# A post-norm decoder layer on one core: key scores and turned-x casts reordered in the first unit of each attention batch

## The reference

```
kv = ln(x) @ kv_w + kv_b ; q = ln(x) @ q_w + q_b      # 16 heads of 32
q, k = rotary(q), rotary(k)                           # radius from x @ rh_w
qn, kn = ln(q), ln(k)                                 # per head
attn = softmax(qn @ kn^T / sqrt(32)) ; a = attn @ v
x = layernorm(x + a @ out_w + out_b)
x = layernorm(x + retention(x, ctx))                  # second phase
x = layernorm(x + coupling_ffn(x))                    # third phase
```

## Time and profile before

| | |
|---|---|
| median of 3 runs | 2026.33 us (2024.2 to 2029.24) |
| the profiled execution | 2028.34 us, of which the span of instructions is 2026.5 us |
| busy share of the span | PE 87%, DVE 73%, ACT 62%, POOL 43% |
| attention, retention, coupling phase | about 1070, 470 and 486 us |
| mean granted clock of TensorE | 0.95 of full speed |

### The profile page before, as it was taken

One profiled execution on the slowest core, in us unless ns is written; L12 is line 12 of the kernel. 1 busy time (PEld: TensorE's weight loads), 2 busy tenths in 40 slices (PEclk: granted clock), 3 DMA queues, 4 the chain that ended last, 5 costly groups with the idle time before them and its releaser, 6 DMA issues. The chain is left out here.

```text
span 2026.5 us, 26481 instructions
## 1 busy us (share of the span) xinstructions
PE 1771.1 (87%) x8648; PEld 1333.6 (66%) x8648; DVE 1477.8 (73%) x2915; ACT 1260.5 (62%) x2674; POOL 867.1 (43%) x802
## 2 busy tenths in 40 slices
PE   6788888988889888898878999999997999999972
PEld 5556665666656666566535888888786777777751
DVE  7768688686876868767655777777764688888876
ACT  3388677787877878777784322222224667777764
POOL 3678668676786767867630222222220000000000
PEclk9799999999999999999978999999998999999986
DMA  4222132321423213222144011111112011111111
GB/s 153 56 80 63 47 110 62 95 64 40 117 62 96 63 46 111 63 73 63 54 144 151 20 54 53 63 63 63 63 59 72 22 42 63 63 63 63 42 42 63
DMA packets 86184, 141.06 MB, mean 70 GB/s; under 512 B 16544, under 2 KB 19616, under 8 KB 86048
## 3 DMA queue, kind: packets, MB, share of 16 engines
q1 hardware_dynamic: 86048, 139.37, 22.7%
HBM read 63.82 MB, written 25.17 MB: 44 GB/s over the span
## 5 line engine op out<-in xcount | busy, mean ns | idle before, releaser
L526 DVE TENSOR_REDUCE a_neg_max<-a_max 128x1 fp32r<-128x512 f32 x512 | 340.6, 685 | 150.5 <-PE a_max L911 148.3
L796 ACT ACTIVATE a_probs<-a_exp 128x512 f32<-128x512 f32 x512 | 294.4, 606 | 206.2 <-PE a_exp L929 205.1
L775 ACT ACTIVATE a_max<-a_max,a_neg_max 128x512 f32<-128x512 f32 x512 | 346.7, 688 | 13.2 <-DVE a_neg_max L526 11.8
L911 PE MATMUL a_max<-a_stack 96*128 96x512 f32 x512 | 220.5, 457 | 85.6 <-ACT a_max L775 77.7
L368 POOL TENSOR_TENSOR a_rstd<-a_rstd,a_minus_half 128x16 f32<-128x16 f32 x64 | 185.9, 2905 | 96.5 <-DVE a_rstd L510 96.4
L886 PE MATMUL a_t<-a_w_hi,a_zT_hi 128*128 128x384 f32 x500 | 183.9, 368 | 36.4 <-DVE a_v L491 27.8
L911 PEld LDWEIGHTS a_max<-a_stack 96*128 96x128 f32 x512 | 99.3, 197 | 175.2 <-ACT a_max L775 130.4
L1717 POOL TENSOR_TENSOR f_yrstd<-f_yrstd,f_minus_half 128x4 f32<-128x4 f32 x8 | 11.0, 1376 | 473.5 <-DVE f_yrstd L1736 473.5
L929 PE MATMUL a_exp<-a_stack 100*128 100x512 f32 x512 | 191.7, 416 | 9.7 <-ACT a_probs L796 6.5
L887 PE MATMUL a_t<-a_w_lo,a_zT_hi 128*128 128x384 f32 x500 | 176.3, 353 | 0.0
L888 PE MATMUL a_t<-a_w_hi,a_zT_lo 128*128 128x384 f32 x500 | 176.1, 352 | 0.0
(11 more groups left out here) (282 smaller groups left out, 4823.6 us busy)
## 6 DMA issues: line engine op xcount, KB each, us to landing
a_stack<-a_nT_hi SPq DMA_DIRECT2D x512, 64.0 KB, 2.0
a_stack<-a_nT_lo SPq DMA_DIRECT2D x256, 64.0 KB, 2.0
a_z<-x SPq DMA_DIRECT2D x8, 1024.0 KB, 7.8
a_y<-x SPq DMA_DIRECT2D x8, 1024.0 KB, 5.6
r_xn<-x SPq DMA_DIRECT2D x8, 1024.0 KB, 5.5
r_cn<-ctx SPq DMA_DIRECT2D x8, 1024.0 KB, 7.8
x<-r_xn SPq DMA_DIRECT2D x16, 512.0 KB, 2.8
f_xn<-x SPq DMA_DIRECT2D x8, 1024.0 KB, 5.5
```

What stands on the lines that cost most here:

```text
L526: nc.vector.tensor_reduce(neg_max[:, t, ROW + h:ROW + h + 1].bitcast(F32R), bank_max[i % NB][:, :], AX_X, ALU.max, negate=True).then_inc(m ...
L775: nc.scalar.activation(bank_max[i % NB][:, :], bank_max[i % NB][:, :], ACT.Exp, bias=neg_max[:, t, ROW + h:ROW + h + 1], accum_out=sums[:, ...
L796: nc.scalar.activation(probs[:, kt % 2, h, :], bank_exp[i % 2][:, :], ACT.Exp).then_inc(exp_done, 1)
L911: mm(bank_max[i % NB][:, :], stack[0:ROW, par, h, t * P:(t + 1) * P], stack[0:ROW, par, HG + h, :], start=True, stop=True).then_inc(score_ ...
```

## The change

Four edits, all in the attention phase:

1. Key scores of units with g=0 come sooner (`KS_DONE` gets a first row), and weighing follows them (`WEIGH_AT`). The exps on ACT follow the same table.
2. In the same units, from slot 1 on, key scores and projections of a slot alternate, a key score first. In slot 0 and in all other units the order stays.
3. Two of the four casts of the turned x and two subtractions are done one slot sooner: tile 0 in slot 12 instead of 13, tile 2 in slot 13 instead of 14.
4. In units with g=1, each tile of the projections waits for its own tile of the turned x. The first two key scores, whose banks hold the turned tiles 2 and 3, get waits of their own.

```
-KS_DONE = tuple(min(4 * (i + 1) // 3, T * HG) for i in range(16))
+KS_DONE = ((2, 5, 7, 8, 9, 10, 11, 12, 13, 14, 15, 16, 16, 16, 16, 16),
+           tuple(min(4 * (i + 1) // 3, T * HG) for i in range(16)))
-WEIGH_AT = (5, 7, 10, 13)
+WEIGH_AT = ((3, 5, 9, 13), (5, 7, 10, 13))
-Z_AT, Z_HIGH_AT, Z_LOW_AFTER = (12, 12, 13, 13), (13, 13, 14, 14), (13, 13, 14, 14)
+Z_AT, Z_HIGH_AT, Z_LOW_AFTER = (12, 12, 13, 13), (12, 13, 13, 14), (12, 13, 13, 14)
...
             def key_scores(U, par, i):
                 kt, h = divmod(i, HG)
                 if i < 2:
+                    if U % G == 1 and U < G * (B - 1):
+                        pe.wait_ge(zlo_done, T * (U // G + 1) + 3 + i)
                     pe.wait_ge(maxrow_saved, 2 * U + i + 1)
...
                 if k == 0:
-                    if m == 0 and g == 1:
-                        pe.wait_ge(zlo_done, T * (b + 2))
+                    if g == 1:
+                        pe.wait_ge(zlo_done, T * (b + 1) + t + 1)
...
+                    items = list(within(PROJECT_DONE, i)) if left >= 3 else []
+                    keys = list(within(KS_DONE[g > 0], i))
+                    if g > 0 or i == 0:
+                        for m in items:
                             project_item(b, g, m)
+                        for m in keys:
+                            key_scores(U, g % 2, m)
+                    else:
+                        for n_item in range(max(len(items), len(keys))):
+                            if n_item < len(keys):
+                                key_scores(U, g % 2, keys[n_item])
+                            if n_item < len(items):
+                                project_item(b, g, items[n_item])
```

More of the change, by code:

```diff
@@ L816, in unit @@
                             sum_exps(U + 1, (g + 1) % 2, m)
-                    for m in within(KS_DONE, i):
+                    for m in within(KS_DONE[g > 0], i):
                         exps(U, m)
@@ L1015, in unit @@
                             query_scores(U + 1, (g + 1) % 2, m)
-                    if left >= 3:
-                        for m in within(PROJECT_DONE, i):
+                    items = list(within(PROJECT_DONE, i)) if left >= 3 else []
+                    keys = list(within(KS_DONE[g > 0], i))
+                    if g > 0 or i == 0:
+                        for m in items:
                             project_item(b, g, m)
[L1019 to L1022, removed]
+                        for m in keys:
[6 more added lines that the diff above has]
+                                project_item(b, g, items[n_item])
+                    if i in WEIGH_AT[g > 0]:
+                        weigh(U, g, WEIGH_AT[g > 0].index(i))
                     if left == 0 and OUT_PART_AT <= i < OUT_PART_AT + T * (G - 1):
```

## The result

| | before | after |
|---|---|---|
| median of 10 runs each, same chip | 2026.72 us (2023.67 to 2031.28) | 2014.49 us (2006.87 to 2019.11) |
| the profiled execution (span) | 2028.34 us (2026.5) | 2008.56 us (2006.8) |
| mean granted clock of TensorE, all runs | 0.9503 | 0.9522 |

The ratio is 0.9936, with a 95% interval of 0.9926 to 0.9947: 12.2 us faster. The runs of this kernel spread roughly with their clock, from 2006.87 us at 0.957 to 2019.11 us at 0.951, but two runs at 0.953 lie 7 us apart (2007.90 and 2014.95), so the mean clock is not all of it.

The account below looks back on a forecast made before the run. No engine is full: PE is close to it in g=0, elsewhere PE, ACT and DVE go round a ring. 6 x 1.1 = 6.6, plus 1.0 and 0.6, gives 8.2 us: 2026.3 - 8.2 = 2018.1 us, own range 2015 to 2022.

Parts of the forecast that it names:

- Start of g=0, 0.46 us: Start of g=0: two more key scores move into PE's wait for DVE's save, taking 0.46 us from the busy part.
- POOL's collision: Start of g=0: DVE's L499 is held beside POOL's L382, 0.49 us instead of 0.17; the 0.32 us stay.
- Weighing sooner, 0.39 - 0.23: Slots 9 and 11 of g=0: the 0.39 us wait for y goes, the heads' wait of 0.16 grows by 0.23.
- The whole term of 0.62 us a batch: Unit g=0, batches 1 to 6: 0.46 + 0.39 - 0.23 = 0.62 us saved by slot 12.
- Turned x, the walk: End of g=0 into g=1, batch 4: tile 3 still waits about 1.9 us; first projection of g=1 starts 1.28 us sooner.
- Turned x, what is kept: Turned x: about 0.5 us a batch kept, making 1.1 us with the 0.62 from g=0.
- upper bound of 1.28: Start of g=1: the batch gains 1.28 us if PE's arrival decides.
- the discount behind it: Start of g=1: DVE's list is full, so DVE follows only 0.3 us where ACT follows the full 1.28.
- the forecast's 1.6 for batches 0 and 7: Batch 0, without out projection: 1.0 us; batch 7, with no turned x to make: 0.6 us.
- The clock stays up at the start of g=0: Rival, chance 0.14: key scores break up the 2.67 us idleness, the clock holds, 10.5 us on top, about 2008.
- the clock falls: Rival, chance 0.09: at the turned x, one-piece idleness ahead of tile 3 halves the clock; 2028.6 or 2039 us.
- The slower rival: Same rival as "the clock falls", at the turned x, chance 0.09: g=1 projections lose 1.5 us per stretch, or 3.

Follow-up runs that it names:

- `keys_fill`: `keys_only` plus unread matmuls in PE's waits (5 at the start of g=0, 4 ahead of the last query score of other units); 1999.54 us, ratio 0.9864.
- `weigh_10`: The changed kernel with only the third weighing moved back from slot 9 to slot 10; 2013.83 us, ratio 0.9934 to the kernel before.
- `x_fill`: `x_only` plus unread matmuls in PE's waits (8 at the start of g=0, 4 ahead of the last query score of other units); 1998.72 us, ratio 0.9854.
- `before_fill`: The kernel before plus unread matmuls in PE's waits (8 at start of g=0, 4 ahead of the last query score of other units); 2007.95 us, ratio 0.9902.
- `after_fill`: The changed kernel plus unread matmuls in PE's waits (5 at start of g=0, 4 ahead of the last query score of other units); 1994.93 us, ratio 0.9838.
- `keys_only`: The changed kernel with only the key score and weighing edits, the turned x as before; 2020.21 us, ratio 0.9961 to the kernel before.
- `x_only`: The changed kernel with only the turned x edits, key scores and weighing as before; 2034.09 us, ratio 1.0033 to the kernel before.
- `no_alternate`: The changed kernel, but projections stand ahead of key scores in each slot of g=0 as before; 2010.24 us, ratio 0.9921 to the kernel before.
- `xrstd_late`: The changed kernel with POOL's step of the next batch's norm moved behind its rotations in units g=3; 2017.54 us, ratio 0.9961 to the kernel before.

## Why the prediction was right, and where it was not

Forecast was 2018.1 us with a range of 2011 to 2025.5; 2014.49 lies in it, and just below the forecast's own range from 2015 to 2022.

- **Start of g=0, 0.46 us.** Three key scores ahead and a stall of 2.2 us in two pieces were forecast, and 0.60 + 1.38 = 1.98 us measured in batch 2. In batch 4 only the 0.60 is left of it, because PE gets there late behind a half-clock stretch. That POOL's collision stays was right as well: L500 takes 0.51 us beside it, as L499 took 0.49.
- **Weighing sooner, 0.39 - 0.23.** Both waits are as forecast: none at the out projection, 0.39 us at the heads. The whole term of 0.62 us a batch measured 0.50 (`keys_fill`). The slot matters for g=0, as the wait that is back in `weigh_10` shows, but not for the time of that run.
- **Turned x, the walk.** The wait of tile 3 was forecast at 1.9 us and is 1.73, for the reason given: the row maxima and the heads' low part stand ahead on DVE. The first projection of g=1 waits for nothing, and ACT's exponential follows 1.22 us sooner, where 1.28 was forecast.
- **Turned x, what is kept. This term was mis-sized.** The sum had "1.1 us as kept by the batch, of which 0.62 come from g=0 and about 0.5 from here". The turned x alone keeps 1.14 us (`x_fill`), and both edits 1.5 to 1.9 in batches 1 to 5, above even the upper bound of 1.28, and 1.1 in batch 6. The walk to the start of g=1 was right: from the first projection of g=0 to that of g=1 `before_fill` takes 42.56 us and `after_fill` 41.19, so 1.37 sooner where 1.28 was forecast. What failed is the discount behind it: DVE's full list was taken to hold part of it back, and all of it was kept. The walk also ended at g=1, while the units behind it gain another 0.5 us net, by the shorter wait in g=2 less the new one in g=3. Added up, batches 1 to 6 keep 9.8 us where the sum had 6.6; with the forecast's 1.6 for batches 0 and 7, which no run separates from the clock, that is about 11 instead of 8.2. The medians of `before_fill` and `after_fill` differ by 13.0 us, of which up to 4 may be clock, since 145 and 137 us at the half level are not the same.
- **The clock, left out of the sum.** It moved in both directions at once. "The clock stays up at the start of g=0" came true in batches 1 to 5, though in three of them the stall was shortened by a half-clock stretch just ahead, and "the clock falls" came true too, in the full change not at the turned x but at the ends of the later units. The two nearly cancel: 201 to 192 us at the half level, which is 4.5 us of the 12.2 if PE is busy throughout. That is an estimate and no bound, since a stretch does not cost the same in every place: against quiet batches with added matmuls, one of 3.4 us costs 1.4 us in batch 4 of the kernel before (126.53 - 123.67, two stretches) and 1.1 in batch 3 of `keys_only` (126.37 - 123.15, three). This may be why `keys_only` gains 7.6 us by steps worth 4, with no less time at the half level; no run tests it. In `x_only` the second wins, and the sign turns. The forecast's reason for the first, that more key scores break up the stall, is not borne out: in `no_alternate` the clock holds in three of six batches behind 2.5 us in one piece, and in the changed kernel it falls in batch 6 behind two. The slower rival's mechanism decided half of the change, `x_only`, and its condition was named too narrowly: the clock also falls at places that the edit does not touch.

So the forecast's nearness is in part luck. A term of 0.5 that was 1.1, and a clock taken as either unchanged or worth 10.5 us, where it was won at one place and paid back at others, were both errors.

What stays open is what, besides a wait, makes the clock fall. Behind 1.73 us of idleness for tile 3 it holds in batches 1 to 6 of the changed kernel; behind 1.74 us in `x_only` it holds in three batches and falls in four. Ahead of it the heads wait 0.39 us in the one and 0.15 in the other; no run here tells what decides. Each kernel has one profile, two for the changed one, and these two differ in the batches in which the clock falls.

## What to carry to other kernels

Read the granted clock of each stretch before and after, next to the waits: an edit that shortens waits can lengthen the program by moving which of them is followed by the half clock, and a part of a change can be slower alone while it is faster in company. To price an edit in a kernel like this, hold the clock first by unread matmuls in its longest waits, and compare units at 1.00; here those matmuls gained more than the edit, 19.9 against 12.2 us. When a small instruction is moved on GpSimd, look at what DVE does in the new place.

## What the runs showed of the hardware

- Matmuls without any use made the program 1.0% faster: 2007.95 us instead of 2027.8, with a mean granted clock of 0.9640 instead of 0.951.
- The half level can follow a wait of 1.63 us in the midst of work: behind it the granted clock was 0.50 for the next 3.4 us, with the weighing at 1.94 us instead of 1.06. Behind the same wait in batch 1 it was 1.00. The Trainium skill (TensorE: Matmul & The Clock Gate, a second HAM failure mode: psum-queue depth-cycling) tells of a bf16 kernel in which TensorE's small idle times between groups of matmuls came often enough to swing the clock between its two levels. This float32 trace fits that at 520.60 and 646.90, but its waits are single ones of over 1.5 us, and no run here varies how often they come.
- The same kernel's ten runs spread over 12 us, the lowest at a mean clock of 0.957 and the highest at 0.951.
- A DVE instruction on 4 numbers a partition took 0.79 us instead of 0.22 beside GpSimd's tensor_tensor, and ended 0.03 us behind it (`xrstd_late`).
